# One 128-row mask matmul per bank in the second block's attention, in place of two on 64 rows

## What is computed

```
q = _rope(q, THETA)
k = _rope(k, THETA)
...
scores = jnp.einsum('bhqd,bhkd->bhqk', q, k) * scale
causal = jnp.tril(jnp.ones((S, S), dtype=bool))
scores = jnp.where(causal[None, None], scores, -jnp.inf)
attn = jax.nn.softmax(scores, axis=-1)
out = jnp.einsum('bhqk,bhkd->bhqd', attn, v)
```

## Time and profile before

| what | us |
|---|---|
| time, median of 3 runs | 4363.69 (4360.85 to 4364.63) |
| profiled execution, its own time | 4355.08 |
| span in that profile | 4353.5 |
| `attention1`, first product to last | 2330 to 3799 |
| busy in the whole span: PE, DVE, ACT, POOL | 3937.5, 3365.8, 2556.4, 1174.0 |
| L2212 busy (DVE) | 1251.7 |
| L2181 busy (ACT) | 1093.8 |
| L2133, L2092, L2111 busy (PE) | 693.5, 436.1, 434.8 |
| L2098 and L2117 busy (PE) | 67.1, 65.4 |

### The profile page before, as it was taken

How to read it: one execution, slowest core, us unless ns; L and a number is a source line. 1 busy time by engine, 2 the same in 40 slices (tenths; PEclk the granted TensorE clock), 3 DMA queues, 4 the chain that set the end, 5 groups by cost and what they waited for, 6 DMA issues and landing times. The chain is left out here.

```text
span 4353.5 us, 97240 instructions
## 1 busy us (share of the span) xinstructions
PE 3937.5 (90%) x39508; PEld 2247.5 (52%) x39508; DVE 3365.8 (77%) x5530; ACT 2556.4 (59%) x3441; POOL 1174.0 (27%) x958
## 2 busy tenths in 40 slices
PE   7999999679998969998986999999999999967996
PEld 4788888546665536665553323233333333334664
DVE  5688888778885558885787889999998988585444
ACT  3566666545553335553423667787888887735553
POOL 1123231267761067771132000000000000013552
PEclk9999999889999989999998989999999999977998
DMA  1011110133320023330044000000000000032444
GB/s 62 6 39 34 36 31 18 45 66 63 63 48 28 0 57 66 62 60 9 0 115 90 9 9 2 5 5 2 9 2 2 9 2 9 4 98 71 91 106 103
DMA packets 290206, 167.13 MB, mean 38 GB/s; under 512 B 204596, under 2 KB 281096, under 8 KB 289288
## 3 DMA queue, kind: packets, MB, share of 16 engines
q1 hardware_dynamic: 267176, 125.49, 13.0%
q0 software_dynamic: 13440, 21.24, 2.7%
q10 hardware_dynamic: 9184, 14.68, 1.0%
HBM read 77.81 MB, written 38.58 MB: 27 GB/s over the span
## 5 line engine op out<-in xcount | busy, mean ns | idle before, releaser
L2212 DVE TENSOR_REDUCE s_tops<-ps 128x2 f32<-128x1024 f32 (+3 forms) x1152 | 1251.7, 1132 | 144.2 <-PE ps L2098 102.6
L2181 ACT ACTIVATE s_weights<-ps 128x1024 f32<-128x1024 f32 (+3 forms) x1152 | 1093.8, 953 | 345.0 <-PE ps L2111 192.6
L2133 PE MATMUL ps<-s_weights,v_flat 128*32 128x256 f32 (+1 forms) x8704 | 693.5, 391 | 7.5 <-ACT s_o_t L2187 6.2
L2111 PE MATMUL ps<-s_q,keys 50*128 50x512 f16 (+3 forms) x2304 | 434.8, 374 | 47.3 <-DVE s_tops L2212 32.9
L2092 PE MATMUL ps<-keys,s_q 48*128 48x512 f16 (+3 forms) x2304 | 436.1, 376 | 44.4 <-DVE s_tops L2212 23.5
L2248 POOL CAST s_shift<-s_minus_top 128x16 f16<-128x16 f32 x32 | 6.3, 198 | 1430.2 <-DVE s_minus_top L2219 1430.2
L583 PE MATMUL ps<-a_qt,a_kt 128*128 128x256 f16 x3072 | 375.3, 273 | 3.8 <-POOL s_ones L538 3.8
L2111 PEld LDWEIGHTS ps<-s_q,keys 50*128 50x128 f16 x2304 | 112.1, 93 | 513.5 <-issue 242.9
L1249 ACT ACTIVATE la_weights<-ps 128x1024 f32<-128x1024 f32 x124 | 126.9, 1023 | 338.2 <-PE ps L1164 338.2
L1174 PE MATMUL ps<-attention_w,la_yt 128*128 128x512 f16 x1152 | 289.2, 399 | 37.9 <-DMA la_yt<-la_y_parts 30.5
L583 PEld LDWEIGHTS ps<-a_qt,a_kt 128*128 128x128 f16 x3072 | 300.7, 98 | 40.5 <-POOL s_ones L538 4.2
(11 more groups left out here) (371 smaller groups left out, 7311.1 us busy)
## 6 DMA issues: line engine op xcount, KB each, us to landing
ex_whole<-in_L_ffn_w_dram ACTq DMA_DIRECT2D x14, 1024.0 KB, 7.2
qk_parts<-a_parts SPq DMA_DIRECT2D x64, 128.0 KB, 3.4
keys<-qk_parts SPq DMA_DIRECT2D x48, 128.0 KB, 5.0
s_q<-qk_parts SPq DMA_DIRECT2D x48, 128.0 KB, 4.8
x<-in_x_dram SPq DMA_DIRECT2D x8, 512.0 KB, 9.2
attention_w<-attention_split SPq DMA_DIRECT2D x2, 2048.0 KB, 9.0
la_table<-in_rotary_dram SPq DMA_DIRECT2D x64, 64.0 KB, 2.1
a_table<-in_rope_dram POOLq DMA_DIRECT2D x8, 512.0 KB, 5.4
```

The costliest lines, as they stand in the source:

```text
L2111: mm = pe.matmul(m.ps[:, bank, skip:CHUNK], m.keys[rows(half, depth), pair, kt * P:(kt + 1) * P], b.q[rows(half, depth), place % 2, pair, ...
L2133: mm = pe.matmul(m.ps[h * QUAD:(h + 1) * QUAD, OUT, begin:end], m.v_flat[:, first:first + QUAD], weights[:, a % 2, h, begin:end], start=(k ...
L2181: act.activation(weights[:, a % 2, 2 * pair:2 * pair + 2, skip:CHUNK], m.ps[:, bank:end + 1, skip:CHUNK], ACT.Exp).then_inc(s["exp"], 1)
L2212: dve.tensor_reduce(tops[:, u % 2, :, i % 2, t, c], m.ps[:, bank:end + 1, 0:width], AX.X, ALU.max).then_inc(s["max"], 1)
```

## The change

The four mask products of a diagonal job become two: for each bank one product of 128 rows, the full identity times the full triangle, streaming 128 columns. Which scores are masked, and with what, stays. The products' form goes from 64*128 to 128*128. POOL builds the three tables whole, with one memset and three selects. `s_upper` goes. Nothing else of the order, the slots or the waits is touched.

```diff
 def attention1_constants(pool, b, done):
-    low, high = slice(0, ROWS), slice(ROWS, P)
-    pool.memset(b.own_row[:, :, :], 0.0)
...
-    for part, own in ((0, low), (1, high)):
-        pool.affine_select(b.own_row[:, part, own], b.own_row[:, part, own], pattern=[[-1, ROWS]], compare_op=ALU.not_equal, fill=1.0,
...
-    pool.tensor_copy(b.later_key_t[high, high], b.upper[high, 1, :]).then_inc(done, 1)
-    pool.wait_ge(done, 5)
+    pool.memset(b.all[:, 0:3 * P], 0.0).then_inc(done, 1)
+    pool.wait_ge(done, 1)
+    pool.affine_select(b.own_row, b.own_row, pattern=[[-1, P]], compare_op=ALU.not_equal, fill=1.0, base=0, channel_multiplier=1)
+    pool.affine_select(b.later_key, b.later_key, pattern=[[-1, P]], compare_op=ALU.is_ge, fill=MASKED, base=0, channel_multiplier=1)
+    pool.affine_select(b.later_key_t, b.later_key_t, pattern=[[1, P]], compare_op=ALU.is_ge, fill=MASKED, base=0,
+                       channel_multiplier=-1).then_inc(done, 1)
+    pool.wait_ge(done, 2)
...
                     if c == j:
-                        for part in range(2):
-                            begin = t * P + part * ROWS
-                            for half, bank in enumerate(banks(("find", i))):
-                                mm = pe.matmul(m.ps[:, bank, begin:width], b.own_row[rows(half, ROWS), part, :], b.later_key[rows(half, ROWS), 0:width - begin],
-                                               start=False, stop=(part == 1))
+                        for bank in banks(("find", i)):
+                            mm = pe.matmul(m.ps[:, bank, t * P:width], b.own_row, b.later_key, start=False, stop=True)
                     mm.then_inc(s["found"], 1)
...
                     if r >= 0:
-                        for part in range(2):
-                            count = (part + 1) * ROWS
-                            for half, bank in enumerate(banks(("score", i))):
-                                mm = pe.matmul(m.ps[:, bank, skip:skip + count], b.own_row[rows(half, ROWS), part, :],
-                                               b.later_key_t[rows(half, ROWS), P - count:P], start=False, stop=(part == 1))
+                        for bank in banks(("score", i)):
+                            mm = pe.matmul(m.ps[:, bank, skip:skip + P], b.own_row, b.later_key_t, start=False, stop=True)
                     mm.then_inc(s["score"], 1)
```

More of the change, by code:

```diff
@@ L1907, in attention1_buffers @@
     b.all = sb("masks", [P, 4 * P], BF16)
[L1908 to L1911, removed]
+    b.own_row, b.later_key, b.later_key_t = (b.all[:, n * P:(n + 1) * P] for n in range(3))
     return b
 def attention1_constants(pool, b, done):
-    low, high = slice(0, ROWS), slice(ROWS, P)
-    pool.memset(b.own_row[:, :, :], 0.0)
-    pool.memset(b.upper[:, :, :], 0.0)
@@ L1920, in attention1_constants @@
[L1920 to L1923, removed]
-    pool.wait_ge(done, 1)
-    for part, own in ((0, low), (1, high)):
-        pool.affine_select(b.own_row[:, part, own], b.own_row[:, part, own], pattern=[[-1, ROWS]], compare_op=ALU.not_equal, fill=1.0,
-                           base=0, channel_multiplier=1)
-    pool.affine_select(b.later_key[:, low], b.later_key[:, low], pattern=[[-1, ROWS]], compare_op=ALU.is_ge, fill=MASKED,
-                       base=0, channel_multiplier=1)
@@ L1930, in attention1_constants @@
[L1930 to L1935, removed]
@@ L1936, in attention1_constants @@
-    pool.wait_ge(done, 2)
[L1937 to L1941, removed]
-    pool.tensor_copy(b.later_key_t[high, high], b.upper[high, 1, :]).then_inc(done, 1)
-    pool.wait_ge(done, 5)
+    pool.memset(b.all[:, 0:3 * P], 0.0).then_inc(done, 1)
```

## The result

The changed kernel takes 4414.42 us (median of 4, 4410.03 to 4415.97) where the kernel before takes 4364.09: a ratio of 1.0113, 95% interval 1.0098 to 1.0128, or +50 us. The forecast was +42 us, 4406.

The account below looks back on a forecast made before the run. ACT's loop paces between diagonals and in diagonal finds; in diagonal scores PE, DVE and that loop nearly coincide. Finds +0.5 and scores +0.9 a unit, 28 x 1.4 = 39, plus 3: +42 us, 4406; range 4380 to 4450.

Parts of the forecast that it names:

- Changes of shape: On PE, each switch between half rows, whole array and few columns costs 0.09 to 0.1 us.
- Rival (a): Half price: whole array to 128*32 is free, so finds cost +0.03, scores still +0.21; time 4381; chance 0.08.
- The step between the two mask products: On PE, from one 128-column mask product to the next: between 0.055 and 0.11 us, taken as 0.055, load hidden.
- Rival (d): Exposed loads: each mask's two whole-array weight loads stand open, +0.2 us more a job; time 4470; chance 0.04.
- Diagonal finds: Finds with diagonal masks: PE +0.12 us each, the loop through ACT grows 0.12 per two rounds, +0.5 us a unit.
- Diagonal scores: Scores with diagonal masks: PE +0.21 us each and PE sets the pace, making DVE late by 0.9 us a unit.
- The rest: First unit's finds without scores, last units' scores without finds, and mixed first units: +3 us in all.
- rival (e): The clock: PE idles 0.2 us more a job; five more falls to the lower level add 25 us, 4431; chance 0.07.
- (b): Hidden: growth falls into PE's existing waits, or shape changes cost nothing around 128-column products; time 4364 to 4368; chance 0.07.
- (c): Faster: half as many mask products and loads to issue saves PE 8 us or somewhat more; time 4354; chance 0.03.

Follow-up runs that it names:

- the run with the mask first: Changed kernel with a diagonal score's mask ahead of its two key products, right behind weigh; 4400.99 us against 4365.65 for the kernel before, ratio 1.0085.
- the run with whole finds alone: Kernel before with two whole-array mask products in the 256 diagonal finds only, scores' masks still four on half rows; 4377.34 us against 4359.14, ratio 1.0041.
- whole scores alone: Kernel before with two whole-array mask products in the 256 diagonal scores only, finds' masks still four on half rows; 4389.62 us against 4359.14, ratio 1.0073.
- 64 columns: Changed kernel with its two whole-array mask products cut to 64 columns each, part of the triangle left unmasked; 4395.64 us against 4359.14 for the kernel before, ratio 1.0086.
- empty products: Kernel before, four masks kept, plus two whole-array products adding zeros to 16 columns in each diagonal find and score; 4423.13 us against 4365.65, ratio 1.0132.

## Why the prediction was right

**Changes of shape**, 0.09 to 0.1 each, whole array to 128*32 included: right. Find to mask grew by 0.09, mask to find holds 0.22, of which 0.12 is the two products. Rival (a), in which the way from whole array to few columns is free, is out: mask to weigh is 0.21, which two products of 0.12 leave 0.09 of.

**The step between the two mask products**: I took 0.055, the lower end of 0.055 to 0.11. The starts of the two products are 0.065 to 0.068 apart, so the step was mis-sized by 0.011. Their weight loads last 0.099, so most of a load is hidden, but not all: in the run with the mask first, 20 masks behind a longer wait of PE have 0.055 between their two products. The step made a score +0.22 to +0.23 in place of +0.21, and a find +0.13 in place of +0.12. The Trainium skill's price for a sustained stream of loads and products at 128 columns ("TensorE: Matmul & The Clock Gate", section "Back-to-back issue gap"), about 81 ns, is above the 66 to 67 ns that two in a row took here. Rival (d), with both loads fully open, is out: it asked for 0.15 or more between the two products. The rule of the Trainium skill that was named with it ("TensorE: Matmul & The Clock Gate", section "The mechanism"), that a load overlaps with running products only when the row groups differ, isn't borne out by the second product of a mask: it needs the same rows, its load of 0.099 begins while the first product streams, and it starts 0.066 behind that one.

**Diagonal finds**: +0.5 a unit forecast. The four pairs of rounds took 2.46, 2.51, 2.57 and 2.66 against 2.32, 2.39, 2.43 and 2.49, +0.57; the run with whole finds alone had +0.57. Right in mechanism: the loop through ACT passes on one find in two.

**Diagonal scores**: +0.9 a unit forecast, 1.09 measured with whole scores alone. This is the term that was short, by 0.2 a unit. The first pair of rounds took 2.89, not 2.82, the second 2.75, not 2.70: the step of 0.066 in each of four jobs, and a weigh of 0.57 to 0.58. DVE's starts are 0.17, 0.24, 0.16, 0.24 and 0.18 further apart than before in the first five rounds, 0.99 together. I had 1.08 less a lead of 0.15 that DVE had at the start. That lead I had read wrongly out of a merged row: in the kernel before, DVE is already kept waiting a little there. Its maxima start 1.13 to 1.14 apart where it has work waiting. From the first of these two to the second it is 1.21, and from there to the next 1.22:

```profile
2639.80 1.22 DVE L2212 TENSOR_REDUCE s_tops<-ps 128x2 f32<-128x1024 f32 x1
2641.01 1.23 DVE L2212 TENSOR_REDUCE s_tops<-ps 128x2 f32<-128x1024 f32 x1
```

For the last three rounds I had no loss, and one of them lost 0.11. PE waits 0.16 and 0.51 there (2666.37, 2668.76). Before it waited 0.68 and then, further on, 0.61:

```profile
2649.27 0.39 PE L2111 MATMUL ps<-s_q,keys 50*128 50x512 f16 x2 [0.61 <-DVE s_tops L2212]
```

So the short last rounds took up their 0.22 each but for that.

**The rest**: +3 for the first and last units was too small. The first four units alone are 10.9 longer, nearly all of it in the two that ran longer at the lower clock. The 28 units behind them are 36 longer, where I had 39 from 28 x 1.4. That this came out so near is in part luck: a usual unit costs 1.7 and not 1.4, but where the chunk changes it costs less, partly because the kernel before has a long fall of the clock there. The remaining 8 us between the two profiles are outside the attention, where one profile against another can't be told from chance; and the profiled execution before is 9 us under its median.

**The clock** (rival (e)): no further falls in the diagonal stretches, and 94 us at the lower level in the attention against 105. But the clock did differ at another place, the start of the attention, where the lower level lasts 58 us against 34. The three other kernels with whole-array products in each diagonal find and score have 72 (64 columns), 55 (mask first) and 120 us (empty products) there, and the seven kernels with half-row products in finds, scores or both, with all masks, have 34 to 38. It is one profile each, so this is a pattern; that the stops keep the clock low isn't shown.

**Hidden** (b) and **faster** (c): the median of +50 us rules out both, and the empty whole-array products, which mask nothing and cost 57 us, say why; four fewer instructions a job bought nothing that shows.

## What to carry to other kernels

In this kernel a product cost a stop of about 0.1 us each time PE went to or from another shape (half rows, whole array, 32 columns), whatever it computed. So try to cut a small product between tiled ones to their shape, even at twice the instructions, and where it can't be cut, put it where the shape changes anyway. The busy time of no group shows such stops; the distance from one start to the next does. Whether they cost anything is read from the stretch. Here the loop through ACT's exponential passed on about half of them in finds. In scores, where PE (2.42), ACT's loop (2.49) and DVE (2.3) lay close together, nearly all were passed on in the first six jobs of a unit, and some 60% over all eight. And a sum that fits can hide its parts: lay the units side by side one by one, with the clock of each.

## What the runs showed that I had not expected

The two whole-array products of a mask start 0.038 to 0.040 us apart at 16 columns as at 64, and mostly 0.066 at 128 columns, with weight loads of 0.099. On half rows a pair of 64 columns is followed by the next pair after 0.03.

Taking 90 ns of PE's work out of each diagonal job made most units without a fall of the clock 0.5 us shorter and yet left the median within 5 us, in two runs, with 43 to 55 us more at the clock's lower level.
